# Mixture-of-experts stage in a fused four-layer kernel: order of the first and second products on TensorE, and a shared ring of two PSUM banks

## The reference, cut to what matters

```python
h = x @ Wm + bm
t = h.reshape(bs * L_ * H, HD)                  # H = 8 heads, HD = 32
logits = t @ expert_emb                         # 16 experts
w = softmax(logits, axis=-1)
topw, topi = top_k(w, 2)
hmid = gelu(einsum('td,edi->tei', t, W1) + b1)  # 32 -> 128, every expert
eo = einsum('tei,eio->teo', hmid, W2) + b2      # 128 -> 32, every expert
sel = take_along_axis(eo, topi[:, :, None], axis=1)
comb = (sel * topw[:, :, None]).sum(axis=1)
return comb.reshape(bs, L_, d) @ Wo + bo        # added to x by the caller
```

## Time and profile before

| | |
|---|---|
| median of 3 runs | 4399.18 us (4398.81 to 4416.64) |
| profiled execution | 4403.25 us, its span 4401.5 us |
| mixture stage | from about 3066 us to the end |
| one steady block | 80.87 us |
| PE busy in a steady block | 78.18 us |
| ACT busy in a steady block | 70.95 us |

### The profile page before, as it was taken

One profiled execution on the slowest core, in us unless ns is written; L12 is line 12 of the kernel. 1 busy time (PEld: TensorE's weight loads), 2 busy tenths in 40 slices (PEclk: granted clock), 3 DMA queues, 4 the chain that ended last, 5 costly groups with the idle time before them and its releaser, 6 DMA issues. The chain is left out here.

```text
span 4401.5 us, 65491 instructions
## 1 busy us (share of the span) xinstructions
PE 4090.3 (93%) x23476; PEld 2398.8 (54%) x23476; DVE 2817.4 (64%) x5635; ACT 2663.8 (61%) x3262; POOL 1548.9 (35%) x1303
## 2 busy tenths in 40 slices
PE   7999999999997899999999989998899999999999
PEld 4444444444444678787878875555344444444443
DVE  6777677776765887878788755544455555554553
ACT  1455555555566554545455424443788888888888
POOL 3122122121223453534344312111344545545545
PEclk7899999999998999999999999999899999999999
DMA  7334234333413224232322320000767666666673
GB/s 188 76 87 101 64 91 97 85 88 79 100 32 113 75 58 115 58 105 68 88 85 70 104 71 5 1 1 6 173 143 165 150 151 161 142 161 158 146 161 89
DMA packets 205761, 429.97 MB, mean 98 GB/s; under 512 B 47584, under 2 KB 72560, under 8 KB 189056
## 3 DMA queue, kind: packets, MB, share of 16 engines
q1 hardware_dynamic: 193360, 411.56, 38.4%
q0 software_dynamic: 4160, 6.35, 0.7%
q10 hardware_dynamic: 7920, 7.87, 0.6%
HBM read 338.59 MB, written 87.03 MB: 97 GB/s over the span
## 5 line engine op out<-in xcount | busy, mean ns | idle before, releaser
L2228 ACT ACTIVATE gelu_out<-hidden,b_col 128x1024 f32<-128x1024 f32 x1024 | 1084.0, 1112 | 163.5 <-PE hidden L2128 162.2
L702 DVE TENSOR_REDUCE maxima<-front 128x1 f32<-128x512 f32 (+3 forms) x1280 | 739.2, 631 | 236.2 <-PE front L509 135.7
L2210 POOL TENSOR_TENSOR combined<-combined,gated 128x512 f32<-128x512 f32 x480 | 617.9, 1287 | 665.5 <-DVE gated L2325 456.5
L601 ACT ACTIVATE probsT<-scoresT 128x1024 f32<-128x1024 f32 (+3 forms) x768 | 585.0, 811 | 287.4 <-PE scoresT L537 282.9
L1160 POOL TENSOR_TENSOR pair_sums<-sims 128x1024 f32<-128x1024 f32 x256 | 481.9, 1903 | 691.9 <-DVEq L1292 433.3
L2325 DVE SCALAR_TENSOR_TENSOR gated<-expert_out,b_col,gates_spread 128x512 f32<-128x512 f32 x480 | 360.3, 751 | 501.7 <-PE expert_out L2138 296.0
L2128 PE MATMUL hidden<-slice_stack,w_stack 128*128 128x512 f32 x2048 | 627.1, 428 | 14.9 <-ACT gelu_out L2228 14.9
L2138 PE MATMUL expert_out<-gelu_out,w_sb 128*32 128x512 f32 x4096 | 548.1, 607 | 24.5 <-DVE gated L2325 13.4
L2128 PEld LDWEIGHTS hidden<-slice_stack,w_stack 128*128 128x128 f32 x2048 | 352.0, 189 | 370.9 <-ACT gelu_out L2228 282.2
L1088 PE MATMUL dense<-xnT,dense_weights 128*128 128x512 f32 x2304 | 538.8, 395 | 8.8 <-ACT silu_down L1194 4.8
L446 POOL TENSOR_SCALAR_AFFINE_SELECT probsT<-probsT 128x512 f32<-128x512 f32 x256 | 161.9, 632 | 1023.6 <-ACT probsT L601 1023.6
(11 more groups left out here) (205 smaller groups left out, 5145.4 us busy)
## 6 DMA issues: line engine op xcount, KB each, us to landing
gates_spread<-gate_scratch SPq DMA_DIRECT2D x512, 256.0 KB, 4.8
dense_weights<-dense_scratch SPq DMA_DIRECT2D x384, 256.0 KB, 2.8
stack_scratch<-split_parts SPq DMA_DIRECT2D x192, 256.0 KB, 3.1
slice_stack<-slice_scratch SPq DMA_DIRECT2D x128, 256.0 KB, 7.6
q_stack<-stack_scratch SPq DMA_DIRECT2D x64, 384.0 KB, 6.1
k_stack<-stack_scratch SPq DMA_DIRECT2D x64, 384.0 KB, 9.1
slice_scratch<-slice_parts SPq DMA_DIRECT2D x32, 512.0 KB, 6.3
out_x<-x_tiles ACTq DMA_DIRECT2D x15, 512.0 KB, 4.9
```

What stands on the lines that cost most here:

```text
L601: nc.scalar.activation(PT[:, i % NPT, 2 * pr:2 * pr + 2, at:BANK], ST[pr][:, :, at:BANK], ACT.Exp, scale=SCALE).then_inc(probs_ready, 1)
L702: nc.vector.tensor_reduce(dst, F[k % 3][:, 0:parts * w].rearrange("p (a k) -> p a k", a=parts), AX.X, ALU.max)\
L2210: nc.gpsimd.tensor_tensor(CM[:, par, hc, :], CM[:, par, hc, :], Y[:, u % 2, :], ALU.add)\
L2228: nc.scalar.activation(GH[:, k % 4, :, :], HP[k % HPB][:, :, :], ACT.Gelu, bias=b1c[:, u % E:u % E + 1])\
```

## The change

Units are taken in **pairs** b: 16 pairs in a block (`BU`), 256 in all (`ALL`). For each pair PE issues the first half and the second half of unit 2b, the first half of unit 2b+1, the front pieces of that pair, the second half of unit 2b+1, and then the second products of units 2b-2 and 2b-1. `GH` gets six buffers instead of four (three units deep), and the gelu of unit n waits for the second products of unit n-3. `OP` and `MB` become two banks `OB` that all second products, front pieces and outputs use in turn: use number i waits for the reader of use i-2. The semaphores `misc_done`, `o_done`, `misc_free` and `y_ready` become `bank_done` and `bank_free`, counted by use.

Front pieces stand at pairs: transposes 0 to 3, projections 4 and 5, logits 6, maxima (now in three parts) 6 to 8, the mask 9, the exponential behind pair 10, three outputs at 11, the fourth at 12, the gates' transposes at 14, the norms for the block after next at 14 and 15. Tiles of `HP` are counted through over all blocks, so the extra wait at a block's start is gone. The logits and softmax buffers (`LS`, `LM`, `EX`, `MK`) now lie in `XN` and `XT`. No product, gelu, gate or add is added or taken away.

```diff
+    GHB = 6
+    BU = NU // 2
+    ALL = NM * BU
...
-        GH = sb("gelu_out", [I, 4, 2, TM])
+        GH = sb("gelu_out", [I, GHB, 2, TM])
...
-        OP = ctx.enter_context(nc.psum_tensor("expert_out", [P, TM], F32))
-        MB = ctx.enter_context(nc.psum_tensor("misc_bank", [P, TM], F32))
+        OB = [ctx.enter_context(nc.psum_tensor(f"out_bank{i}", [P, TM], F32)) for i in range(2)]
...
-        FRONT_AT = dict(zip((0, 1, 2, 3, 4, 5, 6, 7, 8, 9, 10, 11, 12, 13, 18, 19, 20, 22), FRONT))
-        EXP_AT = 14
-        OUTPUT_AT = {15: (0, 1), 16: (2,), 17: (3,)}
+        FRONT_AT = {0: [("x", 0)], 1: [("x", 1)], 2: [("x", 2)], 3: [("x", 3)], 4: [("h", 0), ("s", 0)],
+                    5: [("h", 1), ("s", 1)], 6: [("l", 0), ("m", 0)], 7: [("m", 1)], 8: [("m", 2)], 9: [("d", 0)],
+                    11: [("o", 0), ("o", 1), ("o", 2)], 12: [("o", 3), ("r", 0)], 13: [("k", 0), ("w", 0)],
+                    14: [("g", 0), ("n", 0)], 15: [("n", 1)]}
+        EXP_AT = 10
...
+        def outs(b):
+            return [("e", n, 0) for n in (2 * b - 2, 2 * b - 1) if 0 <= n < NM * NU]
+
+        USES = [(part, 0, t) for part, t in FRONT if part in ON_PE]
+        for b in range(ALL + 1):
+            USES += fronts(b, True) + outs(b) if b < ALL else outs(b)
+        USES += [("o", NM - 1, t) for t in range(TT)]
+        USE = {u: k for k, u in enumerate(USES)}
...
+            def take(*use):
+                if USE[use] >= 2:
+                    pe.wait_ge(bank_free, USE[use] - 1)
+                return bank(*use)
...
+            def hidden(n, p):
+                m, (hc, e) = n // NU, divmod(n % NU, E)
+                if (e, p) == (0, 0):
+                    pe.wait_ge(slices_in[hc], 16 * 4 * (m + 1))
+                k = 2 * n + p
+                if k >= HPB:
+                    pe.wait_ge(gelu_done, k - HPB + 1)
+                for j in range(2):
+                    mm = nc.tensor.matmul(HP[k % HPB][:, j, :], w1s[:, e, :], HS[:, m % 2, G * hc + 2 * p + j, :],
+                                          start=True, stop=True)
+                mm.then_inc(a_done, 1)
+
+            def expert_out(n):
                 pe.wait_ge(gelu_done, 2 * n + 2)
+                ob = take("e", n, 0)
...
+            for b in range(ALL):
+                hidden(2 * b, 0)
+                hidden(2 * b, 1)
+                hidden(2 * b + 1, 0)
+                for part, m, t in fronts(b, True):
+                    front[part](m, t)
+                hidden(2 * b + 1, 1)
+                for _, n, _ in outs(b):
+                    expert_out(n)
...
+            def gelu(n, p):
+                k = 2 * n + p
+                act.wait_ge(a_done, k + 1)
+                if n >= GHB // 2:
+                    act.wait_ge(bank_done, USE["e", n - GHB // 2, 0] + 1)
+                nc.scalar.activation(GH[:, k % GHB, :, :], HP[k % HPB][:, :, :], ACT.Gelu, bias=b1c[:, n % E:n % E + 1])\
+                   .then_inc(gelu_done, 1)
...
+            for b in range(ALL):
+                for part, m, t in fronts(b, True):
+                    front[part](m, t)
+                for _, n, _ in outs(b):
+                    gate_unit(n)
+                for part, m, t in fronts(b, False):
+                    front[part](m, t)
```

More of the change, by code:

```diff
@@ L2114, in output @@
                                           start=(h == 0), stop=(h == HC - 1))
[L2115 to L2130, removed]
@@ L2140, in expert_out @@
                                           tile_position=(0, HD * j))
[L2141 to L2162, removed]
@@ L2164, in _ @@
-            k = 0
+                mm.then_inc(bank_done, 1)
+            front = {"x": turn_x, "h": project, "l": logits, "g": turn_gates, "o": output}
             for part, t in FRONT:
                 if part in ON_PE:
[L2167 to L2171, removed]
+                    front[part](0, t)
+            for b in range(ALL):
[7 more added lines that the diff above has]
+                    expert_out(n)
@@ L2172, in _ @@
+            for _, n, _ in outs(ALL):
+                expert_out(n)
             for t in range(TT):
-                output(NM - 1, 1, t, k + t)
+                output(NM - 1, t)
         @block.gpsimd
@@ L2219, in gate_exp @@
                 act.wait_ge(lm_ready, m + 1)
-                nc.scalar.activation(EX[:, :, :, :], LM[:, :, :, :], ACT.Exp).then_inc(ex_ready, 1)
-            def one_block(m, first, last):
-                for u in range(NU):
-                    for p in range(2):
[L2225 to L2232, removed]
-                        act.wait_ge(misc_free, before(m) + (0 if last else FPB - 1) + TT + 1)
-                        act.dma_start(tiles_out[:, TT * (m - 1):TT * m, :], X[:, TT * (m - 1):TT * m, :])\
-                           .then_inc(stored, 16)
@@ L2237, in _ @@
-            gate_exp(0)
-            for m in range(NM):
-                one_block(m, m == 0, m == NM - 1)
+                nc.scalar.activation(EX, LM, ACT.Exp).then_inc(ex_ready, 1)
+            def gelu(n, p):
[5 more added lines that the diff above has]
+                   .then_inc(gelu_done, 1)
@@ L2266, in split, with logits, maxima @@
                   .then_inc(slices_ready, 1)
-            def logits(m, _, k):
-                dve.wait_ge(misc_done, k + 1)
-                nc.vector.tensor_copy(LS[:, :, :, :], MB[:, :]).then_inc(misc_free, 1)
-            def maxima(m, half, _):
+            def logits(m, _):
+                ob = done("l", m, 0)
+                nc.vector.tensor_copy(flat(LS), ob[:, :].rearrange("p (g e) -> p g e", e=E)).then_inc(bank_free, 1)
+            def maxima(m, part):
                 dve.drain()
-                for t in range(2 * half, 2 * half + 2):
-                    for h in range(H):
-                        nc.vector.max(M8[:, t, h, :], LS[:, t, h, :])
+                for g in range(*MAXIMA[part]):
+                    nc.vector.max(M8[:, g // H, g % H, :], LS[:, g // H, g % H, :])
@@ L2310, in output @@
+            def output(m, t):
                 if t == 0:
                     dve.wait_ge(biased, m + 1)
[L2312 to L2316 removed]
+                ob = done("o", m, t)
+                nc.vector.tensor_tensor(X[:, TT * m + t, :], X[:, TT * m + t, :], ob[:, 0:D], ALU.add)\
+                  .then_inc(bank_free, 1)
```

224 lines of the change are left out of this document (106 added, 118 removed).

## The result

The changed kernel took 4518.93 us (median of 4 runs, 4509.51 to 4521.86) against 4405.66 for the kernel before in the same runs: a ratio of 1.0251, 95% interval 1.0221 to 1.0281. It is slower by 2.5%.

The account below looks back on a forecast made before the run. PE was taken to bound the old kernel at 4.25 us a plain pair; new waits make it 5.0. Blocks, chain and tail sum to +96 us, giving 4495 against a median of 4399.18, range 4445 to 4550.

Parts of the forecast that it names:

- What bounds the kernel before: In the old kernel's stage, PE's stream without gaps: 2.12 us a unit, 4.25 a plain pair; ACT needs only 2.02 a unit.
- Step (a): Fewer changes of product kind per pair: PE's bare stream 3.96 us, ACT's 4.03; without other waits, 4.03 instead of 4.25.
- Step (b): Waits in a plain pair: half 4b+3, second products of unit 2b-2, release, two gelus: 4.99, say 5.0 us, against 4.25.
- The release of ACT by second products: Time from the end of second products to the gelu waiting for them: bounded by 0 and 0.2 us, taken as 0.10.
- the 0.64: From waiting half 4b+3 to the start of second products: 0.56 us plus 0.08 for weights not loaded ahead.
- Step (c): Front pieces ahead of waiting half 4b+3: some 0.5 us of each free; projection adds 1.2, logits 1.3, single output 0.4.
- The gates' transposes vanish: In their pair, the gates' four transpose products, 0.34 us by their number, were to be hidden by PE's wait.
- Step (d): The two-bank ring costs PE nothing and gains at most 24.5 us, the time second products were held up before.
- The gates' way through DRAM: Transposes three pairs, 15 us, ahead of the first product needing them; the spread stays hidden, by little.
- The sum: Over the stage: 14 steady blocks +92, first block -1, last +10, chain before it -2, end outputs -3: +96 us.
- the last block and tail: At the stage's end: last block 83.4 us against 73.20, +10; the four end outputs overlap in twos, -3.
- The clock rival: PE's short gaps lower its clock; if for a quarter of the pairs, mean pair 5.55 us, time 4635; chance 0.08.

Follow-up runs that it names:

- Early: The changed kernel with the second products of unit 2b-2 moved ahead of half 4b+3, the second half of unit 2b+1; 4362.7 us, ratio 0.9905 to before.
- unit: The changed kernel, but each unit's first products are followed by second products of the unit before, front pieces behind the second unit; 4433.15 us, ratio 1.0061 to before.
- unit_ahead: As unit, but front pieces and outputs ahead of unit 2b+1's second half, softmax parts one pair earlier, gates' transposes at pair 13; 4356.45 us, ratio 0.9892 to before.
- gh8: The changed kernel with eight gelu buffers instead of six, slices and gates moved to other buffers for room; 4383.6 us, ratio 0.9952 to before.
- swap: The changed kernel with a pair's second products in the opposite order, unit 2b-1 first, then 2b-2; 4751.53 us, ratio 1.0795 to before.
- behind: The changed kernel with front pieces behind half 4b+3, the second half of unit 2b+1, instead of ahead of it; 4626.27 us, ratio 1.0506 to before.

## Why the prediction was right

*What bounds the kernel before*: PE's stream of 2.12 a unit. Early, unit and unit_ahead show it: a plain pair takes 4.25 again in each, with no gap on PE.

*Step (a)*, a bare stream of about 4.0, was not reached in any plain pair: of the four halves of a burst the last waits for one of three PSUM tiles, and gh8, with the gelu wait gone, took 4.46.

*Step (b)*, the loop, held in every term: 1.16 for 1.17, 0.67 for 0.64, 1.19 for 1.16, 2.02; 5.03 for 4.99. The release of ACT by second products, which no row of before showed, was 0.13 between the bounds 0 and 0.2. The 0.08 for weights in the 0.64 stood in no row either; their sum was right to 0.03. That it is the gelu's wait and not the tile that decides is shown by gh8, swap and early together.

*Step (c)* was right on what the waiting half hides (6.22 for 6.2, 6.29 for 6.3, 5.36 for 5.4, 8.40 for 8.4; 5.03 with a transpose) but wrong on one piece. "The gates' transposes vanish" left out that they need DVE's last softmax step, which had moved behind two gates: 0.65 a block.

*Step (d)*: the ring cost nothing and took the second products' waits from 24.5 to 4.3 us. The 4.3 are with the new order too, so not the ring's alone. The Trainium skill's advice to rotate banks (Perfetto Trace Analysis, section on matmuls) is not contradicted: with order and places mended, the kernel with the ring is 1.1% faster than before, but no run shows the ring's own share. It says nothing of the wait that made this kernel slower. The gates' way through DRAM stayed hidden: DVE waited for no such load in steady blocks. Nor did it in early, with the same three pairs of distance at 4.25; in unit, with two, it did.

*The sum.* The forecast was 4495 in a range of 4445 to 4550, the median is 4518.93. Forecast +96 in the stage, measured 1446.5 - 1334.2 = +112. Steady blocks gave 14 x (88.47 - 80.87) = 106 instead of 92, of which the gates' pair is 9 and the longer loop 5. The chain ahead of the first gelu gave -2.0 for -2 (24.4 us against 26.4), the last block and tail +7.6 (95.2 from its first gelu to the end, 87.6 before) for +7, the first block +0.3 for -1. The parts of the tail held as well: the last block took 84.4 to its last second products for 83.4, and the way from there to the end 12.2 us instead of 15.2, the forecast's -3. The other 6 us between the profiles lie ahead of the stage, where nothing changed.

*The clock rival* did not come: the granted clock was 1.00 in steady blocks, with gaps of 0.28 us on PE twice a pair and one of 1.05 us a block, behind the exponential. What the Trainium skill tells of a kernel with short idle times (TensorE: Matmul & The Clock Gate, section on depth-cycling) does not show in this kernel's steady blocks. Other runs show that it was near. In swap, with gaps up to 0.64 us before it, the clock fell in three of 14 steady blocks; a gap of 2.33 us was followed by the lower clock in 7 of 14 blocks of unit, as in the earlier trace rows, and one of 3.63 in all 14 of behind. So these runs name no length of gap that is safe. A fall of the clock cost 1.6 us each time in swap and 1.0 to 1.6 in unit.

## What to carry to other kernels

A buffer's depth is worth what the order of issue leaves of it: for each wait, ask whether the work it waits for stands ahead of or behind the waiter's own input in the queue of the engine that does both. Grouping more of a kind into a burst moves the consumer's release behind the producer's next input; one call moved ahead of the waiting instruction gave back 156 us here, two further buffers (gh8) 135. Short pieces of other work belong ahead of an instruction that waits anyway, but the inputs of those pieces must then be ready earlier: the gates' transposes that waited for DVE cost 0.65 us a block.

## What was not expected of the hardware

The code ahead of the mixture took up to 22 us more or less between profiles (3056.70 to 3078.52) with no change in it. The intervals of the ratios above reach 0.15% to 0.33% to either side; smaller differences between such kernels are seen in the length of the stage, not in the median. And the granted clock can fall in one block and not in the next with the same instructions and gaps, as in unit: what one stretch of a trace shows of it should be counted over all blocks.
